# A graph layer with routed experts on one core: scattering expert rows straight into the result

## The reference

```
xf = _layernorm(x)                                  # (3125, 256)
top_w, top_i = top_k(xf @ Wg + bg, 2); top_w = softmax(top_w)
for e in range(8):                                  # w_dense: top_w spread over the 8 experts
    h = gelu(xf @ W1[e] + b1[e])                    # 1024 hidden
    out = out + w_dense[:, e:e + 1] * (h @ W2[e] + b2[e])
return x + out
```

## Time and profile before

| | us |
|---|---|
| three runs | 1160.38, 1160.52, 1164.48 |
| median | 1160.52 |
| profiled execution: its time (the only one of the three above its span) | 1164.48 |
| its span, from the first to the last instruction | 1163.6 |
| PE busy | 1056.7 |
| DVE, ACT, POOL busy | 762.1, 623.8, 634.9 |
| mean granted clock of PE, as a share of 2.4 GHz | 0.951 |

### The profile page before, as it was taken

One profiled execution on the slowest core, in us unless ns is written; L12 is line 12 of the kernel. 1 busy time (PEld: TensorE's weight loads), 2 busy tenths in 40 slices (PEclk: granted clock), 3 DMA queues, 4 the chain that ended last, 5 costly groups with the idle time before them and its releaser, 6 DMA issues.

```text
span 1163.6 us, 27165 instructions
## 1 busy us (share of the span) xinstructions
PE 1056.7 (91%) x8001; PEld 1003.1 (86%) x8002; DVE 762.1 (65%) x1942; ACT 623.8 (54%) x1948; POOL 634.9 (55%) x700
## 2 busy tenths in 40 slices
PE   1377999999999999999998977799999999999993
PEld 1267999999999999999997975699999999999992
DVE  6888999999999999999984658333333333333330
ACT  3329555555555555555554760655555555555550
POOL 2474777777777777777731300444444444444431
PEclk9568999999999999999997989899999999999997
DMA  6532333333333333333320334583222222222224
GB/s 160 160 91 68 111 109 112 103 108 103 109 113 105 110 109 109 109 111 105 105 61 5 106 117 181 177 296 65 36 36 34 38 36 36 36 36 36 35 29 124
DMA packets 47378, 108.51 MB, mean 93 GB/s; under 512 B 13814, under 2 KB 24871, under 8 KB 45160
## 3 DMA queue, kind: packets, MB, share of 16 engines
q0 software_dynamic: 30720, 69.24, 24.2%
q1 hardware_dynamic: 16308, 37.47, 9.9%
q10 hardware_dynamic: 308, 1.28, 0.3%
HBM read 90.88 MB, written 20.27 MB: 96 GB/s over the span
## 4 chain that ended last, share of the span: by engine, by line
PE 44%; issue 15%; DVE 12%; POOL 10%; ACT 9%; DVEq 4%; DMA 4%; SPq 0%; POOLq 0%; ACTq 0%
PE ps L961 17%; PE ps L975 16%; POOL xg L556 10%; ACT e L1115 5%; DMA xg<-xn_rows,idx_st 3%; DVEq L1551 2%; PE ps L813 1%; PE ps L864 1%; DVE neg_top L1452 1%; PE ps L860 1%; PE ps L945 1%; ACT agg L1148 1%; PE ps L889 1%; PE ps L699 1%; PE ps L861 1%
## 5 line engine op out<-in xcount | busy, mean ns | idle before, releaser
L556 POOL DMA_INDIRECT xg<-xn_rows,idx_st x416 | 417.5, 1004 | 170.3 <-issue 124.6
L813 PE MATMUL ps<-sel,xg 128*128 128x120 f32 x2496 | 298.5, 276 | 3.8 <-DVE sel L1540 1.3
L813 PEld LDWEIGHTS ps<-sel,xg 128*128 128x128 f32 x2496 | 286.8, 192 | 10.0 <-issue 9.2
L1266 ACT ACTIVATE ht_sb<-ps,b_cur 128x128 f32<-128x128 f32 x448 | 127.9, 369 | 162.5 <-PE ps L961 162.5
L961 PEld LDWEIGHTS ps<-xst,w_st 128*128 128x128 f32 x1792 | 210.1, 193 | 5.6 <-issue 2.8
L961 PE MATMUL ps<-xst,w_st 128*128 128x128 f32 x1792 | 210.6, 276 | 2.3 <-ACT ht_sb L1266 1.7
L1115 ACT ACTIVATE e<-ps,neg_top 128x65 f32<-128x65 f32 x416 | 125.4, 316 | 161.8 <-DVE neg_top L1452 143.7
L975 PE MATMUL ps<-w_sb,ht_sb 128*128 x896 | 202.8, 379 | 0.8 <-DVE y_sb L1845 0.8
L626 POOL DMA_INDIRECT sum_rows<-y_sb,put_st x56 | 108.4, 1935 | 145.6 <-DVE y_sb L1848 135.4
L975 PEld LDWEIGHTS ps<-w_sb,ht_sb 128*128 128x128 f32 x896 | 166.7, 191 | 21.4 <-issue 1.2
L1845 DVE TENSOR_TENSOR y_sb<-ps,b_bc 128x256 f32<-128x256 f32 x56 | 23.8, 425 | 184.2 <-PE ps L975 184.2
(11 more groups left out here) (271 smaller groups left out, 1363.1 us busy)
## 6 DMA issues: line engine op xcount, KB each, us to landing
w_sb<-in_L_ffn_W SPq DMA_DIRECT2D x16, 1024.0 KB, 6.8
xg<-xn_rows,idx_st POOLq DMA_INDIRECT x416
x_sb<-in_x SPq DMA_DIRECT2D x5, 560.0 KB
xn_rows<-xn_sb SPq DMA_DIRECT2D x5, 560.0 KB
xn_t<-xn_rows SPq DMA_DIRECT2D x25, 112.0 KB
expert_in_rows<-xf_sb SPq DMA_DIRECT2D x12, 224.0 KB
sum_rows<-x_sb SPq DMA_DIRECT2D x12, 224.0 KB
out<-sum_rows SPq DMA_DIRECT2D x3, 560.0 KB
```

The costliest lines, as they stand in the source:

```text
L556: pool.indirect_dma_start(xg[:, s, tt, M:M + D], None, xn_dram, bass.IndirectOffsetOnAxis(ap=idx_st[:, s, tt:tt + 1], axis=0)).then_inc(ma ...
L813: mm = pe.matmul(ps3[:, s, col:col + n], xg[:, r, tt, lhs0:lhs0 + 128], sel[:, s, lo:lo + n], start=(tt == 0), stop=(tt == TG - 1))
L1266: ins = act.activation(ht_sb[:, o % 2, c, :], h_of(c), ACT.Gelu, bias=b1_cur[:, o % 2, c:c + 1])
```

## The change

- `sum_rows` is gone. The epilogue writes x to the result tensor `out` itself, and the scatters add to `out`. The ten copies at the end and the two transfers of ones go.
- A padding lane needs another row to add its zero to, and no two lanes of a tile may hit one row. So the kernel finds 128 nodes that are in no expert's last tile. It looks at the first ten nodes of each partition (1250, `SPARES`). POOL marks those whose ranks lie below the last tile of their experts, makes running sums per partition (15 instructions after `slots_ready`), PE adds the counts of the other partitions (`rank_free`, behind round 2), ACT copies them out, POOL makes 0/1 matrices (3 + 10 instructions), PE turns them into 128 node numbers (`place_spares`, two in each round from the sixth), ACT copies those out (behind its first stage_w1), and DVE's `rows_out` makes row 1 of `moves`.
- The loop over PE's rounds is written out.
- `etile` is made ahead of DVE's wait for the last round.
- The first four gathers (`take_first`) read their index from `moves` itself, after the first increment of `moves_ready`. For the first four and last four tiles `put_rows` copies its index ahead of the wait for the previous scatter.
- ACT runs one gelu on one column right behind its exp.

The core of the diff (buffers and semaphores are left out, code is moved left by up to 8 columns):

```diff
@@ -96,12 +96,12 @@
     ROUNDS = K2 * J // COLS
+    SPARES = 10
+    assert SPARES * P >= NE * 128 + 128 and SPARES <= J
     assert ROUNDS * COLS == K2 * J and ROUNDS % 2 == 0
...
     xf_dram = nc.dram_tensor("expert_in_rows", (N, D), F32, kind="Internal").ap()
-    sum_dram = nc.dram_tensor("sum_rows", (N + 128, D), F32, kind="Internal").ap()
@@ -400,8 +414,8 @@
 mix_ps = ps1[0:P, 1, 256:512]
-sum_rows = sum_dram[0:N, :].rearrange("(p j) d -> p j d", j=J)
+spare_ps = ps2[:, 0, 0:512]
 out_rows = out.rearrange("(p j) d -> p j d", j=J)
@@ -480,10 +494,8 @@
         for p0, p1 in ((0, 112), (112, P)):
-            sp.dma_start(sum_rows[p0:p1, tiles[0]:tiles[-1] + 1, :], x_sb[p0:p1, tiles[0]:tiles[-1] + 1, :]) \
+            sp.dma_start(out_rows[p0:p1, tiles[0]:tiles[-1] + 1, :], x_sb[p0:p1, tiles[0]:tiles[-1] + 1, :]) \
                 .then_inc(sum_started, 16)
-    for h in (0, 1):
-        sp.dma_start(sum_dram[N:N + 128, h * 128:(h + 1) * 128], ones[:, :]).then_inc(sum_started, 16)
@@ -500,12 +512,8 @@
+    sp.wait_ge(sum_started, 16 * 2 * NC)
     sp.wait_ge(sum_added, 16 * TILES)
-    for b in range(0, NB, 2):
-        for p0, p1 in ((0, 112), (112, P)):
-            sp.dma_start(out_rows[p0:p1, b * JB:(b + 1) * JB, :], sum_rows[p0:p1, b * JB:(b + 1) * JB, :]) \
-                .then_inc(out_written, 16)
-    sp.wait_ge(out_written, 16 * 2 * NB)
@@ -588,6 +596,8 @@
     pool.wait_ge(staged_rest, 2 * NC)
+    for k in (0, 1):
+        pool.memset(free[:, k, 0:SPARES], 0.0)
     own(pool.memset(below[:, :], 1.0))
@@ -595,16 +605,47 @@
               allow_small_or_imprecise_dtypes=True).then_inc(pairs_numbered, 1)
-    pool.iota(spare_row[:, :], [[0, TILES]], base=N, channel_multiplier=1,
-              allow_small_or_imprecise_dtypes=True).then_inc(pairs_numbered, 1)
+    own(pool.iota(node_no[:, :], [[1, SPARES]], base=0, channel_multiplier=J,
+                  allow_small_or_imprecise_dtypes=True))
+    pool.wait_ge(slots_ready, 1)
+    own(pool.tensor_scalar(last_from[:, :], n_tiles[0:P, 1, :], -1.0, 128.0, ALU.add, ALU.mult))
+    own(pool.tensor_tensor(in_last[:, 0, :, :], ranks[:, 0:SPARES, :],
+                           last_from[:, :].unsqueeze(1).to_broadcast([P, SPARES, NE]), ALU.subtract))
+    own(pool.tensor_scalar(in_last[:, 0, :, :], in_last[:, 0, :, :], 0.0, None, ALU.is_ge))
+    own(pool.tensor_tensor(in_last[:, 1, :, :], picked[:, 0, 0:SPARES, :], picked[:, 1, 0:SPARES, :], ALU.add))
+    own(pool.tensor_tensor(in_last[:, 0, :, :], in_last[:, 0, :, :], in_last[:, 1, :, :], ALU.mult))
+    for w in (4, 2, 1):
+        own(pool.tensor_tensor(in_last[:, 0, :, 0:w], in_last[:, 0, :, 0:w], in_last[:, 0, :, w:2 * w], ALU.add))
+    own(pool.tensor_scalar(free[:, 0, SPARES:2 * SPARES], in_last[:, 0, :, 0], 0.0, None, ALU.is_equal))
+    for k, w in enumerate((1, 2, 4, 8)):
+        a, b = free[:, k % 2, :], free[:, 1 - k % 2, :]
+        own(pool.tensor_tensor(b[:, SPARES:2 * SPARES], a[:, SPARES:2 * SPARES], a[:, SPARES - w:2 * SPARES - w], ALU.add))
+        if k == 0:
+            own(pool.tensor_copy(free_now[:, :], a[:, SPARES:2 * SPARES]))
+    pool.tensor_tensor(free_left[:, :], free[:, 0, SPARES:2 * SPARES], free_now[:, :], ALU.subtract).then_inc(free_ready, 1)
+    pool.wait_ge(free_ranked, 1)
+    own(pool.tensor_scalar(free_rank[:, :], free_rank[:, :], 1.0, None, ALU.add))
+    own(pool.tensor_tensor(free_rank[:, :], free_rank[:, :], free_now[:, :], ALU.mult))
+    own(pool.tensor_scalar(free_rank[:, :], free_rank[:, :], -1.0, None, ALU.add))
+    for c in range(SPARES):
+        ins = pool.tensor_scalar(free_hot[:, c, :], iota_row[:, :], free_rank[:, c:c + 1], None, ALU.is_equal)
+    ins.then_inc(free_hot_ready, 1)
+    def take_first(k):
+        pool.wait_ge(moves_ready, 1)
+        for c in (0, 1):
+            pool.wait_ge(xf_written[c], 32 * ((NC + 1 - c) // 2))
+        pool.indirect_dma_start(xs_sb[:, k, :], None, xf_dram,
+                                bass.IndirectOffsetOnAxis(ap=moves[:, 0, k:k + 1], axis=0),
+                                bounds_check=N - 1, oob_is_err=False).then_inc(xs_loaded[k], 16)
...
         k, s = AT_ONCE * i + o, o % AT_ONCE
-        staged, free = count(pool, k + 1), count(pool, k - AT_ONCE + 1)
-        pool.wait_ge(moves_ready, 2)
-        if past(i) or o >= AT_ONCE:
-            pool.wait_ge(xst_ps, free)
+        staged, freed = count(pool, k + 1 - AT_ONCE), count(pool, k - AT_ONCE + 1)
+        pool.wait_ge(moves_ready, 1)
+        pool.wait_ge(xst_ps, freed)
         pool.tensor_copy(take_st[:, s:s + 1], moves[:, 0, bass.ds(k, 1)]).then_inc(take_staged, 1)
@@ -617,17 +658,19 @@
         pool.wait_ge(moves_ready, 2)
-        if past(i) or o >= 1:
+        if not isinstance(i, int):
             pool.wait_ge(sum_added, count(pool, 16 * k))
         pool.tensor_copy(put_st[:, s:s + 1], moves[:, 1, bass.ds(k, 1)]).then_inc(put_staged, 1)
-        pool.wait_ge(sum_started, 16 * (2 * NC + 2))
+        if isinstance(i, int) and k >= 1:
+            pool.wait_ge(sum_added, 16 * k)
+        pool.wait_ge(sum_started, 16 * 2 * NC)
         pool.wait_ge(y_ready, staged)
         pool.wait_ge(put_staged, staged)
-        pool.indirect_dma_start(sum_dram, bass.IndirectOffsetOnAxis(ap=put_st[:, s:s + 1], axis=0),
+        pool.indirect_dma_start(out, bass.IndirectOffsetOnAxis(ap=put_st[:, s:s + 1], axis=0),
                                 y_sb[:, s, :], None, compute_op=ALU.add).then_inc(sum_added, 16)
     for o in range(AT_ONCE):
-        take_rows(0, o)
+        take_first(o)
     for o in range(AT_ONCE):
@@ -922,11 +965,30 @@
-    for s in (0, 1):
-        place_pairs(0, s)
-    with pe.Fori(1, ROUNDS // 2) as i:
+    def rank_free():
+        pe.wait_ge(free_ready, 1)
+        pe.matmul(spare_ps[0:P, 0:SPARES], below[:, :], free_now[:, :], start=True, stop=False)
+        pe.matmul(spare_ps[0:P, 0:SPARES], ones[0:P, 0:P], free_left[:, :], start=False, stop=True).then_inc(free_counted, 1)
+    def place_spares(c):
+        if c == 0:
+            pe.wait_ge(free_hot_ready, 1)
+            pe.wait_ge(free_ranked, 1)
+        mm = pe.matmul(spare_ps[:, 128:129], free_hot[:, c, :], node_no[:, c:c + 1], start=(c == 0), stop=(c == SPARES - 1))
+        if c == SPARES - 1:
+            mm.then_inc(spares_ps, 1)
+    SPARE_ROUNDS = ROUNDS // 2
+    for i in range(ROUNDS // 2):
         for s in (0, 1):
             place_pairs(i, s)
+            if 2 * i + s == 2:
+                rank_free()
+            if 2 * i + s >= SPARE_ROUNDS:
+                for c in (0, 1):
+                    place_spares(2 * (2 * i + s - SPARE_ROUNDS) + c)
@@ -1242,6 +1304,11 @@
+    act.wait_ge(gap_exp, 1)
+    act.activation(gelu_first[:, :], gap[:, 1, 0:1], ACT.Gelu)
+    act.wait_ge(free_counted, 1)
+    act.activation(free_rank[:, :], spare_ps[0:P, 0:SPARES], ACT.Copy).then_inc(free_ranked, 1)
     act.wait_ge(etile_ready, 1)
@@ -1271,6 +1338,8 @@
     stage_w1(0, 0)
+    act.wait_ge(spares_ps, 1)
+    act.activation(spare_no[:, :], spare_ps[:, 128:129], ACT.Copy).then_inc(spares_ready, 1)
     for k in (0, 1):
@@ -1279,12 +1348,6 @@
-    act.wait_ge(sum_added, 16 * TILES)
-    for b in range(1, NB, 2):
-        for p0, p1 in ((0, 112), (112, P)):
-            act.dma_start(out_rows[p0:p1, b * JB:(b + 1) * JB, :], sum_rows[p0:p1, b * JB:(b + 1) * JB, :]) \
-                .then_inc(out_written, 16)
@@ -1757,7 +1820,9 @@
                                  op0=ALU.mult, op1=ALU.add))
-    own(dve.tensor_tensor(ranks[:, :, :], ranks[:, :, :], row0[:, :].unsqueeze(1).to_broadcast([P, J, NE]), ALU.add))
+    dve.tensor_tensor(ranks[:, :, :], ranks[:, :, :], row0[:, :].unsqueeze(1).to_broadcast([P, J, NE]),
+                      ALU.add).then_inc(slots_ready, 1)
+    dve.wait_ge(slots_ready, 1)
     for k in range(K2):
@@ -1790,30 +1855,33 @@
-    dve.wait_ge(pairs_numbered, 4)
+    dve.wait_ge(pairs_numbered, 3)
     for i in range(ROUNDS // 2):
...
             hots(i, s)
+    own(dve.tensor_tensor(ended[:, :, :], iota_tile[0:1, :].unsqueeze(2).to_broadcast([1, TILES, NE]),
+                          n_tiles[0:1, 1, :].unsqueeze(1).to_broadcast([1, TILES, NE]), ALU.is_ge))
+    own(dve.tensor_reduce(etile_f[:, :], ended[:, :, :], AX.X, ALU.add))
+    dve.tensor_scalar(etile[:, :], etile_f[:, :], float(NE - 1), None, ALU.min).then_inc(etile_ready, 1)
...
     own(dve.tensor_scalar(spare[:, :], placed, 0.0, None, ALU.is_equal))
-    own(dve.tensor_tensor(spare[:, :], spare[:, :], spare_row[:, :], ALU.mult))
     own(dve.tensor_copy(slot_w[:, :], ps1[:, 1, TILES:2 * TILES]))
-    dve.wait_ge(moves_ready, 1)
-    own(dve.tensor_copy(node_f[:, :], moves[:, 0, :]))
-    dve.tensor_tensor(moves[:, 1, :], node_f[:, :], spare[:, :], ALU.add).then_inc(moves_ready, 1)
-    own(dve.tensor_tensor(ended[:, :, :], iota_tile[0:1, :].unsqueeze(2).to_broadcast([1, TILES, NE]),
-                          n_tiles[0:1, 1, :].unsqueeze(1).to_broadcast([1, TILES, NE]), ALU.is_ge))
```

(35 more changed lines are left out.)

2 lines of the change are left out of this document (1 added, 1 removed).

## The result

The changed kernel takes 1165.2 us (median of 20 runs, 1162.1 to 1168.6), the kernel before 1161.7 us in the runs beside them (20 runs, 1159.3 to 1165.1): a ratio of 1.0026, with a 95% interval of 1.0017 to 1.0035. The forecast was 1151.8 us with a range to 1158.5. The range missed: of the gain of 8.75 us that I summed there is nothing, and 3.5 us are lost. (The forecast was counted from 1160.5 us, the median of three executions; with 20 of them the kernel before stands 1.2 us higher.)

The account below looks back on a forecast made before the run. Expert up- and down-projections bound the kernel and stay untouched, so only the two ends count: tail 12.4 plus gather and table 2.35 minus POOL holding DVE 6 gives 8.75 us, median 1160.52 to 1151.8 us; range 1145.5 to 1158.5.

Parts of the forecast that it names:

- The program closes 0.4 after the last landing: Tail: without the ten copies the span ends 0.4 us behind the last scatter's landing; tail gain 12.4 us in all.
- It comes 0.3 less: Tail: the last scatter lands 0.3 us earlier, as its index is copied ahead of its wait.
- Scatters at nothing: Expert stage and tail: scatters aimed at the result instead of sum_rows cost nothing, landing median 4.2 us as before.
- the slower rival of late scatters: Expert stage: scatters into the result land later, up to 121 us lost, 1273 us in all; chance 0.04.
- the 14.75 ahead of the holding: Both ends: the summed gain of 14.75 us before subtracting the time POOL was expected to hold DVE.
- PE 0.7 us: Slot rounds: four more PE passes make a round 0.17 us late, over four rounds 0.7 us.
- POOL holds DVE, turn and turn about, 6 us: Slot rounds: each POOL instruction for spare rows holds DVE for its own length, 6.7 us in all, taken as 6.
- first rival: Slot rounds: POOL and DVE overlap and only PE's passes cost, 0.7 us, giving 1146.5 us; chance 0.27.
- second rival: Slot rounds: POOL starves until DVE stops, PE stands at two new waits; 11.3 us lost, 1157.1 us; chance 0.15.
- Gather and table 2.35: First gather to second up: index read from moves and early gelu table load together gain 2.35 us.
- The spare numbers are covered by the gather: Before the first up: DVE's wait for spare row numbers ends near 729.9 us, before the transpose ends near 731.5.

Follow-up runs that it names:

- e2: The kernel before with only its tail changed (x and scatters into the result, copies gone, no spare rows): 1153.13 us beside 1161.68.
- e4: The changed kernel with seven idle 512-column products on PE ahead of its wait for free_hot_ready: 1159.63 us, ratio to before 0.9986.
- e1: The changed kernel with all ten place_spares moved behind the last round: 1152.95 us beside 1161.68 for the kernel before.
- e7: The kernel before with only gather straight from moves, expert list ahead of the last round and early gelu table load: 1160.45 us beside 1161.28.
- e5: e1 with free_hot made by one DVE instruction behind the last hots and the expert list behind slot_w: 1152.11 us beside 1161.28.

## Why the prediction was wrong, step by step

- **"The program closes 0.4 after the last landing"** failed. I took the 0.4 from a case in which SP was last, and did not ask what the other engines still did under the copies. POOL's drain was in the trace of before, with an end at 1155.7. By the same trace the right sum was at hand: the drain ends 6.9 behind the end of the last scatter's instruction (1148.8), that comes 0.3 earlier, so the end is 1148.8 − 0.3 + 6.9 = 1155.4 for 1163.6, a gain of 8.2. The runs show 7.8 (traces) and 8.6 (e2).
- **"It comes 0.3 less"** held: the last two scatters start 4.54 apart for 4.89. **"Scatters at nothing"** held as well (3.9 for 4.2 to landing, period 7.26), and with it the slower rival of late scatters fell. (Its sum had a slip: a landing of 6.45 us would have cost 55 x 0.26 = 14.3 us, the 14.75 ahead of the holding and not the forecast gain of 8.75.)
- **"PE 0.7 us"** was a little too high. At full clock (e4) a group of four passes lasts 0.52 us, but the rounds come 1.57 to 1.75 apart and the last one ends only 0.2 later for them.
- **"POOL holds DVE, turn and turn about, 6 us"** failed, and it decided the case. From two short copies of POOL that ended with DVE's instruction I concluded a lock that works both ways, though I wrote myself that no row showed DVE held by POOL. It is one-sided: 0.9 us were lost in e1, while POOL's ten instructions took 11.45 for 6.0 alone. In place of the holding the runs show PE itself waiting, 6.0 us at free_hot_ready behind round 5, and then 5.4 us of half clock; with the products moved behind the loop (e1) the rounds neither wait for free_hot nor lose the clock. The Trainium skill (SBUF — State Buffer, Who interferes with whom) says that the two exclude each other for the whole instruction, whichever starts first. POOL's lengthening fits that, DVE's 0.09 us an instruction does not, and the measurement decides. The size of POOL's work was off too: 0.60 us for an instruction of 125x128, where I took 0.30 from one of 125x125 of another kind; part one took 8.0 us (703.36 to 711.36) where I had 3.1.
- The **first rival** (1146.5) was right that DVE is hardly held, but had neither PE's wait nor the drain.
- The **second rival** (1157.1) named the right mechanism at the second of its two waits: PE stands at free_hot_ready behind round 5. The first never bit, since POOL was done with its first part at 711.36, before PE asked at 712.6. Its size for the last round, 11.3, was near the measured 11.9, but by other terms: 6.0 of waiting, 5.4 of half clock, 0.2 of passes and 0.3 ahead of round 5, where I had two waits and a clock left alone. That the two numbers are near each other is luck. That it gave no gain at all needed the clock and the drain besides; with the middle as measured and the drain it would have read 1160.5 − 8.2 + 11.2 = 1163.5, outside my range, which had only "a part of a slower clock".
- **"Gather and table 2.35"** held as mechanism: 0.84 behind moves, no load at the gelus, and 1.9 by e7's trace. In the changed kernel only 0.7 is left of it. The clock was down before the first `up` began and came back only 1.2 us before its end: 6.18 for 5.19. The gather's instruction, beside DVE's weight copy, took 1.67 for 1.06. The clock, which I left "as it was", was the larger term here.
- **"The spare numbers are covered by the gather"** held (spare_no at 737.36, transposes at 741.61).

So in place of 12.4 + 2.35 − 6 = 8.75 the traces have 7.8 from the tail and, from the middle, 0.7 − 11.9 = −11.2 to the second `up`, of which 10.6 are left at the last scatter.

## What to carry to other kernels

An engine that sees work end in the shadow of a longer tail still has its own end: before the tail is cut, read what every engine closes with. A small product put into the middle of a paced loop makes the whole loop wait for its slowest producer, and an idle TensorE pays twice, by the wait and by the clock after it. Put such work behind the loop, where a transfer's flight covers it (e1: 12 us for a move of three lines), and look for an engine that does it in one instruction (1.48 us of DVE in e5 for 11.45 of POOL in e1, though the medians don't tell the two kernels apart).
